# Block transposes of a graph kernel in two halves of 64 partitions each, with two rows sharing two PSUM banks

## What is computed

```python
def _L0_gnn_ref(x, W, U, w_scale):          # x (8, 2048, 64), W = adj (8, 2048, 2048), U (2048, 16)
    Ws = 0.5 * (W + jnp.swapaxes(W, -1, -2))
    A = jax.nn.sigmoid(U @ U.T)
    K = Ws * A[None, :, :]
    deg = jnp.maximum(K.sum(axis=-1), EPS)
    d = jax.lax.rsqrt(deg)
    K = K * d[:, :, None] * d[:, None, :]
    return w_scale * jnp.einsum('bnm,bmc->bnc', K, x)

x = _layernorm(x + _L0_gnn_ref(x, adj, L0_gnn_U, L0_gnn_w_scale), axis=-1)
```

## Time and profile before

| | |
|---|---|
| median of 3 runs | 522.15 us (521.48 to 524.45) |
| profiled execution | 525.09 us, its span 523.3 us |
| busy: PE, VectorE (DVE), ScalarE (ACT), GpSimd (POOL) | 497.5, 426.6, 218.4, 112.7 us |
| matmul records on PE | 3208 |
| from HBM | 138.5 MB, mean 273 GB/s |

### The profile page before, as it was taken

One profiled execution on the slowest core, in us unless ns is written; L12 is line 12 of the kernel. 1 busy time (PEld: TensorE's weight loads), 2 busy tenths in 40 slices (PEclk: granted clock), 3 DMA queues, 4 the chain that ended last, 5 costly groups with the idle time before them and its releaser, 6 DMA issues.

```text
span 523.3 us, 10251 instructions
## 1 busy us (share of the span) xinstructions
PE 497.5 (95%) x3208; PEld 307.7 (59%) x3208; DVE 426.6 (82%) x1137; ACT 218.4 (42%) x654; POOL 112.7 (22%) x132
## 2 busy tenths in 40 slices
PE   3899999999999999999999999999999999999891
PEld 3686646765466645765567655676466754766330
DVE  5898766999697987999878987999779986999433
ACT  2996413553154432544136432544234541554300
POOL 0000010024400351015400343004410244003611
PEclk9999999999999999999999999999999999999897
DMA  8999699768989499867999579895998589890011
GB/s 241 387 329 377 241 356 369 225 226 295 373 310 305 162 325 385 286 208 291 346 325 312 211 283 371 308 277 199 346 389 269 209 285 373 305 332 19 2 41 40
DMA packets 102852, 142.99 MB, mean 273 GB/s; under 512 B 37296, under 2 KB 37296, under 8 KB 102832
## 3 DMA queue, kind: packets, MB, share of 16 engines
q1 hardware_dynamic: 88240, 139.08, 75.6%
q10 hardware_dynamic: 14592, 3.67, 3.2%
HBM read 138.54 MB, written 4.19 MB: 273 GB/s over the span
## 4 chain that ended last, share of the span: by engine, by line
PE 81%; SPq 6%; DMA 5%; DVE 3%; issue 3%; POOLq 0%; POOL 0%; ACT 0%; DVEq 0%
PE yp L365 38%; PE tw L336 20%; PE kt L350 19%; SPq L190 6%; DMA k<-in_adj_dram 3%; PE yp L446 3%; DMA out_dram<-h 2%; DVE k L558 1%; PE yp L384 1%; DVE k L548 1%; SPq L195 1%; POOLq L111 0%; POOL rstd L314 0%; DVE mean L599 0%; DVE z L578 0%
## 5 line engine op out<-in xcount | busy, mean ns | idle before, releaser
L466 ACT ACTIVATE k<-kt 128x512 f32<-128x512 f32 (+3 forms) x288 | 151.9, 528 | 255.5 <-PE kt L350 250.9
L548 DVE TENSOR_TENSOR k<-tw,k 128x512 f32<-128x512 f32 (+2 forms) x320 | 193.4, 605 | 59.5 <-PE tw L336 49.9
L365 PE MATMUL yp<-k,z 128*64 128x512 f32 x928 | 215.2, 600 | 1.7 <-DVE z L578 1.7
L558 DVE CUSTOM_DVE_ANT_0 k<-k,gate 128x512 f32<-128x512 f32 (+2 forms) x320 | 208.2, 651 | 0.3 <-ACT gate L457 0.3
L336 PE MATMUL tw<-ident,k 128*128 128x128 f32 x1088 | 170.8, 274 | 0.9 <-ACT ut_b L522 0.7
L350 PE MATMUL kt<-ident,k 128*128 128x128 f32 x960 | 155.0, 277 | 3.2 <-DVE deg_parts L558 2.5
L350 PEld LDWEIGHTS kt<-ident,k 128*128 128x128 f32 x960 | 110.7, 140 | 50.6 <-issue 41.9
L336 PEld LDWEIGHTS tw<-ident,k 128*128 128x128 f32 x1088 | 127.4, 140 | 20.0 <-DVE k L548 13.8
L365 PEld LDWEIGHTS yp<-k,z 128*64 128x64 f32 x928 | 60.1, 136 | 104.9 <-issue 104.4
L264 POOL TENSOR_TENSOR d<-deg,minus_half 128x4 f32<-128x4 f32 x32 | 32.4, 1013 | 237.3 <-DVE deg L568 236.5
L466 ACT ACTIVATION_READ_ACCUMULATOR k<-kt 128x1 f32 x288 | 57.0, 198 | 0.0
(11 more groups left out here) (60 smaller groups left out, 122.6 us busy)
## 6 DMA issues: line engine op xcount, KB each, us to landing
k<-in_adj_dram SPq DMA_DIRECT2D x128, 1024.0 KB, 7.2
xt<-in_x_dram ACTq DMA_DIRECT2D x7, 512.0 KB, 6.5
out_dram<-h SPq DMA_DIRECT2D x7, 512.0 KB, 9.3
xt<-in_x_dram SPq DMA_DIRECT2D x1, 512.0 KB, 14.6
out_dram<-k SPq DMA_DIRECT2D x2, 256.0 KB, 2.6
h<-in_L_gnn_U_dram SPq DMA_DIRECT2D x1, 128.0 KB, 5.2
ws<-in_L_gnn_w_scale_dram ACTq DMA_DIRECT2D x1, 0.5 KB, 3.2
```

The lines of the kernel that those rows point to most:

```text
L365: t = pe.matmul(yp[at:at + C, m // 2, :], z[:, n * G + c, :], K[(n, m)][:, c, :], start=(q == first_unit[m] and c == 0), stop=(q == last_u ...
L466: nc.scalar.activation(K[(j, i)][:, r, c0:UW], kt[:, g % KT_RING, 0:UW - c0], ACT.Copy, accum_out=deg_parts[:, n, part:part + 1]).then_inc ...
L548: nc.vector.tensor_tensor(row, tw[:, tw_bank[g], 0:w], row, ALU.add).then_inc(sum_done, 1)
L558: nc.vector.tensor_tensor_reduce(row, row, A[:, A_AT[g]:A_AT[g] + w], 1.0, 0.0, ALU.mult, ALU.add, deg_parts[:, i * G + r, j:j + 1]).then_ ...
```

## The change

Each block of 128 x 128 is transposed by two instructions in place of one. The first takes partitions 0 to 63 of the block and of the identity, the second partitions 64 to 127; each gives 128 partitions x 64 columns. The two halves are written to two different banks. Two neighbouring rows share these two banks: bank h holds half h of every block, the first row in its columns 0 to 255, the second row in 256 to 511. So TensorE waits once for two rows, and issues both; `tw` is now two pairs of banks, `kt` one pair. VectorE and ScalarE read a row from both banks in runs of 64 columns, and wait until both rows of the pair are transposed, because the banks are shared. The wait for free banks is carried by an instruction of its own, `sem_inc(banks_taken)`. Upper rows are issued in pairs as well, at the even one's place. Products, the transposes of y, the first outer products and every size of data stay.

```diff
--- before.py
+++ after.py
@@ -13,7 +13,9 @@
 
 P = 128
 G = 4
+H = P // 2
 UW = G * P
+HALF_ROW = UW // 2
 DEG_EPS = 1e-12
 LN_EPS = 1e-5
 
@@ -146,6 +148,16 @@
         kt = ctx.enter_context(nc.psum_tensor("kt", [P, KT_RING, UW], F32))
         yp = ctx.enter_context(nc.psum_tensor("yp", [P, 2, UW], F32))
         tw_bank = [g % TW_RING for g in range(NL)]
+
+        def tw_banks(g):
+
+            return [tw[:, tw_bank[g] // 2 * 2 + h, :] for h in range(2)]
+
+        def whole_rows(t, slot, chunks):
+
+            return (t[:, :, HALF_ROW * slot:HALF_ROW * slot + H * chunks]
+                    .rearrange("p h (c e) -> p c h e", e=H))
+
         assert NL % TW_RING == 0 and NU % KT_RING == 0
 
         def h_last(k):
@@ -162,6 +174,7 @@
         uu_done, gate_ready = sem("uu_done"), sem("gate_ready")
         tw_done, sum_done, lower_done = sem("tw_done"), sem("sum_done"), sem("lower_done")
         kt_done, upper_done = sem("kt_done"), sem("upper_done")
+        banks_taken = sem("banks_taken")
         deg_summed, deg_ready, d_ready, z_ready = sem("deg_summed"), sem("deg_ready"), sem("d_ready"), sem("z_ready")
         prod_done, y_copied, yt_done = sem("prod_done"), sem("y_copied"), sem("yt_done")
         f_ready, y_scaled, h_ready = sem("f_ready"), sem("y_scaled"), sem("h_ready")
@@ -325,17 +338,26 @@
                     last = max(n for n in range(NL) if tw_bank[n] == tw_bank[g])
                     pe.wait_ge(sum_done, b * NL + (last + 1 - NL))
 
+            def transpose_halves(dst, at, blocks):
+
+                for k, block in enumerate(blocks):
+                    for h in range(2):
+                        t = pe.transpose(dst[h][:, at + k * H:at + (k + 1) * H], block[H * h:H * h + H, :],
+                                         ident[H * h:H * h + H, H * h:H * h + H])
+                return t
+
             def transpose_adjacency(b, s, r, first):
 
                 i, j = STEPS[s]
-                g = s * G + r
                 if r == 0:
                     pe.wait_ge(loaded[(j, i)], b * 16 + 16)
-                bank_free(b, g, first)
-                for c in range(lower_width(s, r) // P):
-                    t = pe.transpose(tw[:, tw_bank[g], c * P:(c + 1) * P], K[(j, i)][:, c, r * P:(r + 1) * P],
-                                     ident[:, :])
-                t.then_inc(tw_done, 1)
+                bank_free(b, s * G + r + 1, first)
+                pe.sem_inc(banks_taken, 1)
+                for row in (r, r + 1):
+                    g = s * G + row
+                    transpose_halves(tw_banks(g), HALF_ROW * (g % 2),
+                                     [K[(j, i)][:, c, row * P:(row + 1) * P] for c in range(lower_width(s, row) // P)]
+                                     ).then_inc(tw_done, 1)
 
             def transpose_rows(b, s, r, first):
 
@@ -343,13 +365,13 @@
                 g = UPPER.index((s, r))
                 if r == 0:
                     pe.wait_ge(lower_done, b * NL + G * (s + 1))
-                if not first or g >= KT_RING:
-                    pe.wait_ge(upper_done, b * NU + (g + 1 - KT_RING))
-                chunks = range(G) if i != j else range(r + 1, G)
-                for k, c in enumerate(chunks):
-                    t = pe.transpose(kt[:, g % KT_RING, k * P:(k + 1) * P], K[(i, j)][:, c, r * P:(r + 1) * P],
-                                     ident[:, :])
-                t.then_inc(kt_done, 1)
+                if not first or g:
+                    pe.wait_ge(upper_done, b * NU + g)
+                pe.sem_inc(banks_taken, 1)
+                for row in range(r, min(r + 2, upper_rows(s))):
+                    transpose_halves([kt[:, h, :] for h in range(2)], HALF_ROW * (row % 2),
+                                     [K[(i, j)][:, c, row * P:(row + 1) * P]
+                                      for c in (range(G) if i != j else range(row + 1, G))]).then_inc(kt_done, 1)
 
             def product(b, q, c, first):
 
@@ -401,12 +423,13 @@
 
             def uppers_at(b, row, lag, first):
                 for up in UPPER:
-                    if due(row, lag, upper_row_of(*up)):
+                    if up[1] % 2 == 0 and due(row, lag, upper_row_of(*up)):
                         transpose_rows(b, *up, first)
 
             def steps(b, lags):
                 for row in range(NL):
-                    transpose_adjacency(b, *LOWER[row], lags == 1)
+                    if row % 2 == 0:
+                        transpose_adjacency(b, *LOWER[row], lags == 1)
                     for lag in range(lags):
                         for k in range(2):
                             if due(row, lag, Y_ROWS[k]):
@@ -462,8 +485,9 @@
                 g = UPPER.index((s, r))
                 c0, part = (0, i) if i != j else (P * (r + 1), 4)
                 n = j * G + r
-                act.wait_ge(kt_done, b * NU + (g + 1))
-                nc.scalar.activation(K[(j, i)][:, r, c0:UW], kt[:, g % KT_RING, 0:UW - c0], ACT.Copy,
+                act.wait_ge(kt_done, b * NU + (g - r % 2 + min(2, upper_rows(s) - r // 2 * 2)))
+                nc.scalar.activation(K[(j, i)][:, r, c0:UW].rearrange("p (c h e) -> p c h e", h=2, e=H),
+                                     whole_rows(kt[:, 0:2, :], r % 2, (UW - c0) // P), ACT.Copy,
                                      accum_out=deg_parts[:, n, part:part + 1]).then_inc(upper_done, 1)
 
             def copy_y(b, k, first):
@@ -541,11 +565,12 @@
             def add_row(b, g):
                 s, r = LOWER[g]
                 w = lower_width(s, r)
-                row = K[STEPS[s]][:, r, 0:w]
+                row = K[STEPS[s]][:, r, 0:w].rearrange("p (c h e) -> p c h e", h=2, e=H)
                 if r == 0:
                     dve.wait_ge(loaded[STEPS[s]], b * 16 + 16)
-                dve.wait_ge(tw_done, b * NL + (g + 1))
-                nc.vector.tensor_tensor(row, tw[:, tw_bank[g], 0:w], row, ALU.add).then_inc(sum_done, 1)
+                dve.wait_ge(tw_done, b * NL + (g // 2 * 2 + 2))
+                nc.vector.tensor_tensor(row, whole_rows(tw[:, tw_bank[g] // 2 * 2:tw_bank[g] // 2 * 2 + 2, :], g % 2, w // P),
+                                        row, ALU.add).then_inc(sum_done, 1)
 
             def gate_product(b, g, first):
                 s, r = LOWER[g]
```

## The result

The kernel became slower. Four runs have a median of 533.87 us (527.15 to 536.75), against 523.09 us for four runs of the kernel before (521.48 to 524.45): a ratio of 1.017, 95% interval 1.0087 to 1.0252. So the loss is clear of the noise, its size (1 to 2.5%) is not. The forecast was 494 us, with a range of 480 to 528. The profiled execution took 527.15 us, its span 525.3; it is the lowest of the runs, so its windows can explain only the smaller part of the loss: its span is 2.0 us longer than before, the median 10.8.

A forecast was written before the change was run, and what follows sets the result against it. PE was taken to set the pace, VectorE close behind. Seven batches 4.2 us shorter (29.4) and the first +1 took 28.4 off the median of 522.2: 494 us (493.8), range 480 to 528.

The forecast's parts named there:

- A block: PE's transposes: two halves run side by side, 0.06 us a block instead of 0.109, saving 12.5 us a batch.
- the change of shape: On PE, between halves and products or y: the array drains, 0.15 us each, 0.6 us a batch.
- the add: VectorE's add reading runs of 64 columns over two banks: should stay at 684 ns.
- the last part of the prediction: Signs to check: PE idle before upper pairs (released by ACT) and before lower pairs (by VectorE's add).
- Both signs: Forecast wrong if the first batch grows by over 6 us, or PE sits at new waits while VectorE starves.
- ACT's turn stays just under VectorE's pace, and where products follow the upper pair it is hidden: Between upper pairs, PE waits for ScalarE's two reads: 2.0 us a pair against VectorE's 2.43, or hidden under products.
- about 237.3: Start of row 37's products on PE in the walked batch, instead of 238.54: gain 1.2 us.
- The walk: One loop batch followed through VectorE's waits: 8.3 us fall to about 3.9, the batch some 4.2 us shorter, to 56.
- +1 us, between -2 and +6: First batch's change in time: up to 8.1 us of shape changes against 10.6 saved on transposes.
- (c): Rival, chance 0.12: halves work, but pair waits, ACT's turn of 2.4 and DMA waits leave 1 us a batch; 512 to 520.
- (a): Rival, chance 0.13: halves don't overlap and coarser pairs cost PE time; batch 66 to 67 us, about 565 in all.

The follow-up runs named there:

- the short copies: Changed kernel with ScalarE copying only the first block of every upper row, three quarters of these copies left out: 509.68 us, ratio 0.974.
- The filler: Changed kernel with each lower half transposed twice in the ten pairs of a batch without products: 539.59 us, ratio 1.033.

## Why the prediction was wrong

**Right.** A block costs 0.064 us (0.06 was taken), the change of shape 0.14 (0.15), the add 684 ns. PE's work in a batch fell from 60.4 to 50.2 us, 10.2 where 11.9 were forecast (12.5 less 0.6); the waits before upper pairs, for ScalarE, stand where the last part of the prediction put them. Both signs by which it would know itself wrong came true: the first batch grew by 9.8 us, more than 6, and PE sits at the new waits (61.5 us) while VectorE starves (56.2).

**The step that failed first: "ACT's turn stays just under VectorE's pace, and where products follow the upper pair it is hidden".** Both sides of that comparison were off. The turn was put at 2.0 us and is 2.16 (360.71 to 362.87). ScalarE's timeline:

```profile
361.46 0.60 ACT L489 ACTIVATE k<-kt 128x512 f32<-128x512 f32 x1 [0.90 <-PE kt L345]
...
362.05 0.59 ACT L489 ACTIVATE k<-kt 128x512 f32<-128x512 f32 x1
```

It starts reading 0.75 after the pair's first transpose (0.68 was put), and PE goes on 1.41 after that (1.3 was put). More important, VectorE's pace was taken from full rows, 2.43 for two. At the diagonal rows the upper pairs are full and VectorE's rows are short:

```profile
359.15 0.28 DVE L572 TENSOR_TENSOR k<-tw,k 128x128 f32<-128x128 f32 x1
...
363.25 0.28 DVE L572 TENSOR_TENSOR k<-tw,k 128x128 f32<-128x128 f32 x1
...
365.39 0.42 DVE L572 TENSOR_TENSOR k<-tw,k 128x256 f32<-128x256 f32 x1
...
367.80 0.56 DVE L572 TENSOR_TENSOR k<-tw,k 128x384 f32<-128x384 f32 x1 [1.04 <-PE tw L345]
```

From row 32 (359.15) to row 36 (363.25) it needs 4.10 us, 2.05 a pair: less than the turn. In exactly these rows PE must get ahead, because row 37's products hold it for 3.6 us. Here they start at 363.52, 0.27 after VectorE began row 36; before they started at 238.54, when VectorE was at row 34 (the add of row 36 came at 240.03). PE had a lead of 1.5 us there and has none now: 1.8 less, where the prediction had these products 1.2 us earlier ("about 237.3"). So row 38 waits 1.04, and in the batch before it, whose products ran at the lower clock, 2.73.

The walk had row 2's wait at 0.3: it is 1.81 (315.33, where 1.34 stood in the earlier trace rows). Little of that comes from row 37, for with its calls moved the wait is still 1.42. The walk let the products of row 41 wait for z alone and so start 1.7 us ahead of row 0 (243.7 against 245.44). Before them stands one more upper row, and it waits for ScalarE too, when z (365.93, 0.82 us long) has long been made:

```profile
369.20 0.28 PE L345 MATMUL kt<-ident,k 64*128 64x64 f32 x2 [0.89 <-ACT k L489]
```

The products follow at 369.41, 0.3 ahead of row 0 (369.73). With the short copies this wait is still 0.52 us, and row 2's 1.49. The wait that the walk put before row 10 was 1.7, and 1.82 is there (329.46); the load's is 0.80 (320.06), as put. Against the walk VectorE thus waits 1.0 us more before row 38 and 1.5 more before row 2, 2.5 together, where the batch (58.3) is 2.3 longer than forecast. In the loop, then, it is one thing at two places: ScalarE's turn ahead of the products of row 37 and of row 41. The short copies bear it out: with a turn of 1.5 a batch takes 56.7.

**The step that failed second: the first batch, "+1 us, between -2 and +6".** It was counted in changes of shape against transposes saved; the pairs weren't counted at all, and they cost 8.0 us there with whole blocks. VectorE's adds show where. From row 0 to row 28 it takes 34.6 us before, 39.0 with pairs of whole blocks and 39.1 in the changed kernel; from there to the next batch's row 0 15.2, 18.8 and 20.5. So about half of the loss lies in the rows in which the products of U and the gate are made, the rest behind them.

In the first part ScalarE also makes the gate. Its timeline, with the upper pairs of PE at 27.00 and 30.14:

```profile
27.75 0.60 ACT L489 ACTIVATE k<-kt 128x512 f32<-128x512 f32 x1
...
28.34 1.08 ACT L480 ACTIVATE gate<-yp 128x512 f32<-128x512 f32 x2
29.30 0.61 ACT L489 ACTIVATE k<-kt 128x512 f32<-128x512 f32 x1
...
29.86 0.62 ACT L480 ACTIVATE gate<-yp 128x512 f32<-128x512 f32 x1
```

Two activations of the gate, 0.96 us, stand between the two reads of a pair, so the turn is 3.14 us, well over VectorE's 2.43. Before, PE filled one bank while ScalarE read the other, and the gate's work lay beside that. In the second part it is row 37 again: VectorE waits 5.20 us before row 38 (71.01), 4.78 with pairs of whole blocks, and waited 2.65 before. That the pairs cost this time is shown; that they do it through ScalarE's turn is argued, and for the first part only in part: with the short copies PE waits 1.4 us for ScalarE in this batch instead of 6.5 and row 38 2.64, but row 28 still comes 39.5 us after row 0, at the lower clock for much of it.

**The sum.** The span was forecast at 494.9 and is 525.3. The first batch took 59.6 instead of 50.8 (+8.8), the seven others 412.9 instead of 392 (+20.9), the end 39.5 instead of 38.1 (+1.4), and the start came 0.8 earlier; together 30.3. Of the 20.9, 15.7 go with the short copies (412.9 less 397.2); 1.7 of them may be one set of products at the lower clock (5.35 us instead of 3.65). The other 5.2 stay with short copies too and aren't settled. The median, 533.87, lies 40 us over the forecast. 30 of them are these; 2.9 come from the profiled run having been taken to lie that much above the median, as before the change, and 6.7 from its lying below it. Where the 6.7 are lost no window shows.

**The rivals.** (c) named ScalarE's turn, but with other work coming between ("0.8 a row instead of 0.6"), which in the loop rows shown it doesn't. It left a gain of 1 us a batch, and 1.2 were in fact left; it forgot the first batch. (a) had the price of the pairs, and its condition, no overlap, didn't hold. In the profiled run seven batches gain 8.4 us, so the change loses as soon as the first batch loses more; the prediction weighed the two against each other nowhere.

**Open.** The runs of the changed kernel, with one more than the four above, go in the order of their granted clock: 0.971, 0.962, 0.958, 0.958 and 0.953 with 527.15, 532.71, 533.86, 533.87 and 536.75 us. The kernel before has 0.986 to 0.993. That would fit a second cost of a PE that pauses, through the clock, the 7 us of the median over the profiled run among it; but the same numbers would come about if what makes a run long also made its clock fall. The filler raised the clock and cost time, and so doesn't tell them apart. Nor is the order strict in other kernels: with the first batch whole, runs at 0.978 took 522.71 and 526.17 us.

## What to carry to other kernels

When two buffers that were filled in turn become one that is filled and read as a pair, work out the full turn (fill, wake-up, both reads, release, and whatever the reader does between its reads). Hold it against the consumer's pace in every kind of row, the lightest first, and in the first stage, where other work shares the reader. An engine that is made faster must still arrive early at its long, indivisible piece of work; count its lead there, before and after, rather than its busy time. A stage with other work on the same engines may be left as it was: here that alone turned a loss into no change, and with four calls moved into a gain of 2%.

## What the runs showed of the hardware

- Two transposes that take 64 partitions each, from different halves, run side by side: a block of fp32 took 0.064 us against 0.109 whole, where two halves of 64 columns, 0.054 each, would take 0.109 one after another. Sixteen loads of 128 columns started within 0.49 us, 31 ns each on average. Single starts in the trace show two patterns. In some groups they follow each other at about this distance (360.68), in others they come in pairs 3 to 4 ns apart, as forecast, a pair about every 58 ns (45.04).
- To change the shape of the matmuls cost 0.14 us on TensorE, from halves to products (0.65 against 0.51 us) and from halves to whole transposes.
- TensorE's granted clock fell to its lower level (1.2 of 2.4 GHz) in the middle of the work. This window of the changed kernel's first batch has a granted clock of 0.51, with PE busy for 6.42 of 7.00 us; in the 6 us ahead of it PE had paused three times, for 0.78 us at most:

```profile
17.00:24.00 7.00, 6.42 (x53) 4.21 (x54) 5.63 (x15) 3.46 (x9) 0.00 (x0) 0.51 1.06 388
```

- At the lower clock sixteen matmuls of products took 5.04 us (65.35) and 5.35 (303.47), where 3.65 is usual. The profiled execution of the kernel before has no such stretch ahead of 488 us.
